# A kernel of two layers: masks added on VectorE, part of a normalisation on ScalarE

## What is computed

```python
q = _rope(qkv[:, :, :HQ], pos); k = _rope(qkv[:, :, HQ:HQ + HKV], pos); v = qkv[:, :, HQ + HKV:]
k = jnp.repeat(k, rep, axis=2); v = jnp.repeat(v, rep, axis=2)
scores = jnp.einsum('bqhd,bkhd->bhqk', q, k) * D ** (-0.5)
causal = jnp.tril(jnp.ones((s, s), dtype=bool))
scores = jnp.where(causal[None, None], scores, jnp.finfo(scores.dtype).min)
attn = jax.nn.softmax(scores, axis=-1)
out = jnp.einsum('bhqk,bkhd->bqhd', attn, v).reshape(b, s, HQ * D)
return jnp.einsum('bso,ho->bsh', out, w_o)
```

## Time and profile before

| | |
|---|---|
| median of 3 runs | 380.17 us (379.9 to 381.06) |
| profiled execution | 380.05 us, its span 378.2 us |
| granted TensorE clock | 0.999 |
| busy: TensorE, VectorE, ScalarE, GpSimd | 95%, 81%, 66%, 75% |
| chain that ended last | TensorE 80%, VectorE 11%, ScalarE 4% |

### The profile page before, as it was taken

One profiled execution on the slowest core, in us unless ns is written; L12 is line 12 of the kernel. 1 busy time (PEld: TensorE's weight loads), 2 busy tenths in 40 slices (PEclk: granted clock), 3 DMA queues, 4 the chain that ended last, 5 costly groups with the idle time before them and its releaser, 6 DMA issues.

```text
span 378.2 us, 8305 instructions
## 1 busy us (share of the span) xinstructions
PE 360.5 (95%) x2808; PEld 335.7 (89%) x2824; DVE 307.1 (81%) x684; ACT 250.7 (66%) x804; POOL 282.3 (75%) x242
## 2 busy tenths in 40 slices
PE   8999988997899999999999999999999999999995
PEld 3668878997898999999999999999999999998984
DVE  6868998866999987879878887887787878888882
ACT  1367865563987666777767586867666777767771
POOL 5537759789999999999779697777987977775000
PEclk9999999999999999999999999999999999999999
DMA  7997001523343445343345743343455433334100
GB/s 258 412 409 314 28 30 45 144 66 83 85 109 97 118 118 149 101 121 87 83 114 143 178 114 103 102 105 85 126 136 162 122 85 85 84 100 105 50 2 28
DMA packets 35371, 46.19 MB, mean 122 GB/s; under 512 B 4609, under 2 KB 27138, under 8 KB 34946
## 3 DMA queue, kind: packets, MB, share of 16 engines
q1 hardware_dynamic: 35184, 45.66, 41.8%
q10 hardware_dynamic: 146, 0.00, 0.0%
HBM read 13.14 MB, written 1.05 MB: 38 GB/s over the span
## 4 chain that ended last, share of the span: by engine, by line
PE 80%; DVE 11%; ACT 4%; DMA 2%; issue 2%; POOL 0%; SPq 0%
PE bank L1321 17%; PE bank L1033 13%; PE bank L1341 12%; PE bank L1229 12%; PE bank L1281 10%; PE bank L1188 3%; PE bank L1287 3%; PE bank L1284 2%; ACT bank L519 2%; PE bank L1164 2%; PE bank L1042 2%; DMA wq0T<-in_L_attn_w_qkv_dram 2%; PE bank L1245 2%; DVE neg_max L940 1%; PE bank L1050 1%
## 5 line engine op out<-in xcount | busy, mean ns | idle before, releaser
L519 ACT ACTIVATE bank<-bank,neg_max 128x256 f32<-128x256 f32 (+1 forms) x256 | 101.1, 396 | 10.5 <-DVE neg_max L940 10.3
L528 ACT ACTIVATE probT_hi<-bank 128x512 fp32r<-128x512 f32 x96 | 57.7, 602 | 65.0 <-PE bank L1033 64.9
L940 DVE TENSOR_REDUCE neg_max<-bank 128x2 f32<-128x512 f32 (+1 forms) x96 | 65.9, 687 | 23.6 <-PE bank L1287 13.2
L1321 PE MATMUL bank<-probT_hi,v 128*128 128x256 f32 x384 | 76.5, 295 | 0.7 <-DVE oT_lo L968 0.7
L956 DVE TENSOR_TENSOR prob<-bank,rsum 128x512 f32<-128x512 f32 x96 | 66.4, 691 | 3.3
L962 DVE TENSOR_TENSOR probT_lo<-bank,probT_hi 128x512 fp32r<-128x512 f32 x96 | 65.3, 681 | 0.5 <-ACT probT_hi L528 0.4
L681 POOL TENSOR_TENSOR rope_b<-turned,cst 128x512 f32<-128x512 f32 x36 | 46.9, 1302 | 22.1 <-DMA turned<-raw 22.1
L1281 PE MATMUL bank<-kT,qT 128*128 128x256 f32 (+1 forms) x384 | 62.6, 272 | 0.0
L1033 PE MATMUL bank<-cst,prob 128*128 128x128 f32 x384 | 57.9, 273 | 4.3 <-DVE prob L956 3.3
L1321 PEld LDWEIGHTS bank<-probT_hi,v 128*128 128x128 f32 x384 | 58.7, 189 | 3.6 <-issue 2.3
L1281 PEld LDWEIGHTS bank<-kT,qT 128*128 128x128 f32 x384 | 55.0, 191 | 0.0
(11 more groups left out here) (163 smaller groups left out, 781.7 us busy)
## 6 DMA issues: line engine op xcount, KB each, us to landing
turned<-raw SPq DMA_DIRECT2D x72, 128.0 KB, 2.0
qT<-q_hi SPq DMA_DIRECT2D x64, 128.0 KB, 2.4
qT<-split_lo SPq DMA_DIRECT2D x64, 128.0 KB, 2.4
wq0T<-in_L_attn_w_qkv_dram SPq DMA_DIRECT2D x4, 512.0 KB, 7.9
wout<-in_L_attn_w_out_dram SPq DMA_DIRECT2D x4, 512.0 KB, 12.7
nat_qkv<-in_L_attn_w_qkv_dram SPq DMA_DIRECT2D x2, 1024.0 KB, 20.4
nat_o<-in_L_attn_w_o_dram SPq DMA_DIRECT2D x1, 2048.0 KB, 21.1
kT<-split_hi SPq DMA_DIRECT2D x16, 128.0 KB, 2.4
```

The lines of the kernel that those rows point to most:

```text
L519: ins = nc.scalar.activation(own, own, ACT.Exp, bias=neg_max[it % 2][:, first + j:first + j + 1], accum_out=sums[it % 2][:, first + j:firs ...
L528: nc.scalar.activation(probT[0][:, n % 4, :], bank[2 + n % 2][:, :], ACT.Copy).then_inc(t_hi, 1)
L940: dve.tensor_reduce(neg_max[n // UNITS % 2][:, unit_columns(n % UNITS)], score_bank(n)[:, :].rearrange("p (h k) -> p h k", h=heads), AX.X, ...
L1321: ins = pe.matmul(group_bank(), v[b % 2][:, DH * z:DH * z + P], p, start=m == 0, stop=m == last)
```

## The change

The queries' rotation constants are negated, so that the scores come out negative. The maximum becomes a minimum, which needs no negation to be the exponential's bias, and the exponential takes its input with scale -1. The mask becomes +1e30. In the constants a block of zeros (C_FREE) stands ahead of the mask, so that both together are a mask of 256 columns.

For units with c = 1 TensorE's mask matmul is left out; the last scores matmul signals s_full. VectorE adds the mask itself, head by head, in place in the bank, with an instruction that also takes the minimum (`tensor_tensor_reduce`, add and min, with accumulator output). Units with c = 0 keep the mask matmul and the one reduction.

The table SHARED = (0, 4) names the units of a pass whose product with the reciprocal ScalarE does (`shares`), one instruction per head; VectorE does only the reciprocal there. `normed` is TensorE's wait for whichever engine did it.

```diff
--- before.py
+++ after.py
@@ -25,14 +25,14 @@
 EPS_LN, EPS_BIT = 1e-5, 1e-6
 EPS_RMS = float(np.finfo(np.float32).eps)
 MAGIC = 1.5 * 2.0 ** 23
-MASKED = -1e30
+MASKED = 1e30
 WQ0_PIECES = 4
 ITS = B * HKV
 UNITS = 6
 N_UNITS = ITS * UNITS
 
 
-C_ID, C_MASK, C_EVEN, C_ONE, C_QC = (P * i for i in range(5))
+C_ID, C_FREE, C_MASK, C_EVEN, C_ONE, C_QC = (P * i for i in range(6))
 C_QS, C_KC, C_KS, C_ALL = (C_QC + SEQ * i for i in range(1, 5))
 
 
@@ -49,8 +49,8 @@
     ang = np.arange(SEQ, dtype=np.float32)[None] * np.tile(np.repeat(inv, 2), P // DH)[:, None]
     sign = np.where(np.arange(P) % 2, np.float32(1), np.float32(-1))[:, None]
     cos, sin = np.cos(ang).astype(np.float32), np.sin(ang).astype(np.float32) * sign
-    c[:, C_QC:C_QC + SEQ] = cos * np.float32(DH ** -0.5)
-    c[:, C_QS:C_QS + SEQ] = sin * np.float32(DH ** -0.5)
+    c[:, C_QC:C_QC + SEQ] = cos * np.float32(-(DH ** -0.5))
+    c[:, C_QS:C_QS + SEQ] = sin * np.float32(-(DH ** -0.5))
     c[:, C_KC:C_KC + SEQ] = cos
     c[:, C_KS:C_KS + SEQ] = sin
     return c
@@ -172,6 +172,7 @@
         ld_qkv = [sem(f"ld_qkv_{i}") for i in range(3)]
         s_dve = sem("s_dve")
         yT_in, full_done, x_hi, xr_done = sem("yT_in"), sem("full_done"), sem("x_hi"), sem("xr_done")
+        s_norm_act = sem("s_norm_act")
         w_hi, w_lo = sem("w_hi"), sem("w_lo")
         root_in, root_out = sem("root_in"), sem("root_out")
         const_done = sem("const_done")
@@ -264,6 +265,16 @@
             else:
                 engine.wait_ge(raw_done, BLOCK[f] + 1)
 
+        SHARED = (0, 4)
+
+        def normed(engine, n):
+
+            upto = [m % UNITS in SHARED for m in range(n + 1)]
+            if upto[n]:
+                engine.wait_ge(s_norm_act, upto.count(True))
+            else:
+                engine.wait_ge(s_norm, upto.count(False))
+
         def unit_heads(u):
 
 
@@ -516,9 +527,22 @@
                 first = unit_columns(u).start
                 for j in range(heads):
                     own = score_bank(n)[:, wide * j:wide * j + wide]
-                    ins = nc.scalar.activation(own, own, ACT.Exp, bias=neg_max[it % 2][:, first + j:first + j + 1],
+                    ins = nc.scalar.activation(own, own, ACT.Exp, bias=neg_max[it % 2][:, first + j:first + j + 1], scale=-1.0,
                                                accum_out=sums[it % 2][:, first + j:first + j + 1])
                 ins.then_inc(s_exp, 1)
+
+            def shares(n):
+
+                act.wait_ge(rs_done, n + 1)
+                if n >= 3:
+                    act.wait_ge(t_full, n - 2)
+                _, heads, _, wide = unit_heads(n % UNITS)
+                first = unit_columns(n % UNITS).start
+                for j in range(heads):
+                    own = slice(wide * j, wide * j + wide)
+                    ins = nc.scalar.activation(prob[n % 3][:, own], score_bank(n)[:, own], ACT.Copy,
+                                               scale=rsum[n // UNITS % 2][:, first + j:first + j + 1])
+                ins.then_inc(s_norm_act, 1)
 
             def probs_T(n):
 
@@ -535,6 +559,8 @@
             def slot(n):
                 if 2 <= n < N_UNITS + 2:
                     probs_T(n - 2)
+                if 1 <= n < N_UNITS + 1 and (n - 1) % UNITS in SHARED:
+                    shares(n - 1)
                 if n < N_UNITS:
                     probs(n)
                 if group_at(n):
@@ -936,10 +962,16 @@
 
             def maxima(n):
                 dve.wait_ge(s_full, n + 1)
-                _, heads, _, _ = unit_heads(n % UNITS)
-                dve.tensor_reduce(neg_max[n // UNITS % 2][:, unit_columns(n % UNITS)],
-                                  score_bank(n)[:, :].rearrange("p (h k) -> p h k", h=heads),
-                                  AX.X, ALU.max, negate=True).then_inc(s_max, 1)
+                c, heads, _, wide = unit_heads(n % UNITS)
+                own = neg_max[n // UNITS % 2][:, unit_columns(n % UNITS)]
+                if c:
+                    for j in range(heads):
+                        part = score_bank(n)[:, wide * j:wide * j + wide]
+                        ins = dve.tensor_tensor_reduce(part, part, cst[:, C_FREE:C_FREE + SEQ], 1.0, 3e38, ALU.add, ALU.min,
+                                                       accum_out=own[:, j:j + 1])
+                else:
+                    ins = dve.tensor_reduce(own, score_bank(n)[:, :].rearrange("p (h k) -> p h k", h=heads), AX.X, ALU.min)
+                ins.then_inc(s_max, 1)
 
             def normalise(n):
 
@@ -949,6 +981,8 @@
                 par = n // UNITS % 2
                 dve.reciprocal(rsum[par][:, own], sums[par][:, own]).then_inc(rs_done, 1)
                 dve.wait_ge(rs_done, n + 1)
+                if n % UNITS in SHARED:
+                    return
                 share = rsum[par][:, own].rearrange("p (h k) -> p h k", k=1).to_broadcast([P, heads, wide])
                 if n >= 3:
                     dve.wait_ge(t_full, n - 2)
@@ -1267,7 +1301,7 @@
                 if u == 0 and g == 0:
                     has_landed(pe, BLOCK["k", b])
                 if n >= 3:
-                    pe.wait_ge(s_norm, n - 2)
+                    normed(pe, n - 3)
                 elif n == 0:
                     pe.wait_ge(f_gelu, TILES - 1)
                 elif n == 2:
@@ -1278,17 +1312,17 @@
                     pe.wait_ge(pad_zero, 2 * (b + 1))
                 for j in range(heads):
                     for s in range(c + 1):
-                        pe.matmul(ps[:, keys * j:keys * j + keys], qT[it % 2][:, h + j, P * c:P * c + P], kT[b % 2][:, g, s, 0:keys],
-                                  start=j == 0 and s == 0, stop=False, skip_group_check=True)
+                        ins = pe.matmul(ps[:, keys * j:keys * j + keys], qT[it % 2][:, h + j, P * c:P * c + P], kT[b % 2][:, g, s, 0:keys],
+                                        start=j == 0 and s == 0, stop=bool(c and s), skip_group_check=True)
                     if c == 0 and j % 2:
                         pe.matmul(ps[:, keys * (j - 1):keys * (j + 1)], q_hi[it % 2][:, (h + j) // 2, 0:P], k_pad[b % 2][:, g, :, :],
                                   start=False, stop=False, skip_group_check=True)
-                diag = ps[:, :].rearrange("p (h k) -> p h k", h=heads)[:, :, P * c:P * c + P]
-                pe.matmul(diag, ident_b[:, :], mask_b[:, 0:heads, :], start=False, stop=True,
-                          skip_group_check=True).then_inc(s_full, 1)
+                if c == 0:
+                    ins = pe.matmul(ps[:, :], ident_b[:, :], mask_b[:, 0:heads, :], start=False, stop=True, skip_group_check=True)
+                ins.then_inc(s_full, 1)
 
             def prob_T(n):
-                pe.wait_ge(s_norm, n + 1)
+                normed(pe, n)
                 if n >= 2:
                     pe.wait_ge(t_lo, n - 1)
                 elif n == 0:
```

## The result

The change is slower: 387.06 us (median of 4 runs, 386.8 to 388.13) against 380.03 us (4 runs, 379.79 to 381.06), a ratio of 1.0185, 95% interval 1.0169 to 1.0202. Predicted were 386.3 us and slower, with a range of 379.0 to 392.0. The profiled execution took 386.95 us with a span of 385.1 (before 378.2): 6.9 us to explain.

What follows compares the result with a forecast made beforehand. TensorE, busy 95% of the span, bounds the kernel, with its waits for oT_lo. Ordinary passes +1.1, k 0, v +2.6, pass 0 +1.0, pass 1 +0.6, pass 15 +0.6 and +0.4: +6.3 us, forecast 386.3, range 379.0 to 392.0.

Steps and rivals of the forecast that it cites:

- one chain in unit 5: Extreme values through shares, exponentials and oT_lo to TensorE's third head group: 3.71 us, was 2.67; growth 1.04 exceeds slack 0.73.
- k passes: Passes 5 and 9, k projection in unit 4: wait of 0.49 us against 0.48 won, net 0.
- v passes: Passes 2, 6, 10, v projection in unit 4: wait 1.33 us, net +0.85 each, +2.6 for three.
- ordinary passes: Eight passes (3, 4, 7, 8, 11 to 14): wait 0.43 us, 0.36 won, net +0.14 each, +1.1 us.
- rival 2: Chain in unit 5 shorter than worked, break-even at 3.37 us; with lower bounds -1.6 us, 378.5 us; chance 0.16.
- Extreme values: VectorE's two add-and-minimum instructions per unit: 0.37 + 0.08 us each, 0.90 for the unit, +0.31 over one reduction.
- Rival 1: VectorE's pairs of instructions don't overlap: 1.14 us instead of 0.90, +6.0 us, 392.3 us; chance 0.10.
- Shares: ScalarE's two scaled copies of 256 elements, PSUM to SBUF: 0.36 us apart, 0.72 for the pair.
- Rival 3: ScalarE's copies cost 0.45 us each: +2.9 us, 389.2 us; chance included in the forecast's 0.66.
- Passes 0 and 1: Pass 0 +1.0 us, only unit 4's mask won; pass 1 +0.6, after 0.3 off for VectorE's relief.
- shares of unit 0: ScalarE's copies in unit 1's slot, costed at nothing: done 2.3 us after the scores end, needed some 2.7 after.
- Pass 15: Last pass: wait of 0.90 us runs through to the end, +0.6 net; VectorE's lateness at unit 0's transposes +0.4.

Runs made afterwards that it cites:

- e1: The change with no shared units: VectorE does all products with the reciprocal and still adds the c = 1 masks; 379.75 us, ratio 0.998 to the kernel before.
- e4: The change with TensorE's mask matmul back in all units, units 0 and 4 still shared; 385.73 us, ratio 1.0143 to the kernel before.
- e3: The change with unit 4 alone shared on ScalarE; 385.69 us, ratio 1.0141 to the kernel before.
- e2: The change with unit 0 alone shared on ScalarE; 379.08 us, ratio 0.9976 to the kernel before.
- e8: The change with masks on VectorE only from pass 3 on and no shares on ScalarE; 377.35 us, ratio 0.9913 to the kernel before.
- e9: The full change, masks and shares, but only from pass 3 on; 381.76 us, ratio 1.0042 to the kernel before.
- e5: The change with unit 4's shares issued behind oT_hi instead of ahead of unit 5's exponentials; 383.93 us, ratio 1.009 to the kernel before.
- e6: The change with the shares of both unit 4 and unit 0 issued later in ScalarE's order; 389.94 us, ratio 1.0236 to the kernel before.

## Why the prediction came out right, and where its terms were off

**The mechanism held.** The prediction put everything on one chain in unit 5, and on the slack of 0.73 us behind it. The chain was found as written, the waits stand where they were named (unit 0 in nearly every pass, longest after a v projection), and e1, with the masks alone, has none in unit 0 of the ordinary and k passes and 0.4 us in the v passes. In ordinary passes e4, with the shares alone, has none there either: that wait takes both. Length of the chain to the start of oT_lo: before 2.10 us, predicted 3.14, measured 2.98. With oT_lo and the signal that is 3.55 us for 3.71, above the 3.37 us at which rival 2 let the change break even.

**Extreme values, 0.90 us predicted, 0.72 measured.** The term that failed is the 0.08 us for each read of the accumulator; the 0.37 for each instruction was right. In the trace a read starts together with the next instruction, and takes no time of its own: the steps are 0.34 and 0.38 us, though each instruction lasts 446 ns. Rival 1 falls with it. The Trainium skill, VectorE: DVE Perf Modes, section The DRAIN you can't avoid, has the next operation wait until the pipe is empty, and adds that one that is not held back starts earlier; here the second starts 0.08 us before the first one's end, so it is the addition that the trace agrees with. This takes some 0.2 us from each wait: 0.23 measured for 0.43 in ordinary passes, 0.31 for 0.49 in the k passes, 1.15 for 1.33 in v passes. So the ordinary passes came out at 0, not +0.14 each (0.2 us for the eight, predicted 1.1), the k passes at -0.3 for two (0), the v passes at +2.0 for three (+2.6).

**Shares, 0.72 us predicted, 0.73 measured.** Taken from the step of two exponentials' lengths, and right. The Trainium skill, ScalarE: Activation LUTs, section What ACT_TABLE_LOAD costs, gave an estimate of 0.40 us apart; the trace has 0.365, 0.73 for the pair. Rival 3, 0.45 each, falls with that.

**Passes 0 and 1, +1.6 us predicted, +3.2 measured.** The failed step is the 0.3 us "from VectorE's relief" and the silence on VectorE's own additions there. VectorE isn't relieved: its feed-forward instructions get longer, and the extreme values come late behind them. In the change, GpSimd, VectorE and ScalarE at the seam of the two passes:

```profile
109.16 1.58 DVE L1017 SCALAR_TENSOR_TENSOR x<-wcol,ffac,x 128x256 f32<-128x256 f32 x1
109.17 1.30 POOL L723 TENSOR_TENSOR split_lo<-rope_a,q_hi 128x512 fp32r<-128x512 f32 x1
...
110.67 0.42 DVE L970 CUSTOM_DVE_ANT_0 bank<-bank,cst 128x256 f32<-128x256 f32 x1
...
111.39 0.15 DVE L982 RECIPROCAL rsum<-sums 128x2 f32<-128x2 f32 x1
...
111.59 0.84 ACT L543 ACTIVATE prob<-bank,rsum 128x256 f32<-128x256 f32 x2 [1.30 <-DVE rsum L982]
```

The reciprocal of unit 0 stands behind an instruction of 1.58 us and the extreme values, and the transposes wait 1.34 us for the shares (112.48, above). That is not ScalarE's doing. In e3 VectorE makes the same product, and TensorE waits as long:

```profile
112.22 0.42 PEld L1067 LDWEIGHTS bank<-cst,prob 128*128 128x128 f32 x4 [1.33 <-DVE prob L990]
```

So the shares of unit 0, costed at nothing, cost next to nothing here too: e2 and e1 are 0.04 us apart in the two passes together, the change and e3 0.14. e1 and e2 divide the loss of 3.2 us: masks alone cost 1.85 in the two passes, with unit 0's shares it is 1.9, and unit 4's shares make up the rest.

**Pass 15, +1.0 us predicted, +0.7 measured;** the 0.4 us for unit 0's transposes didn't come.

**The last store, 0 predicted, +1.1 measured.** The prediction has no term for it.

**The total was partly luck.** Too little was forecast for passes 0 and 1 (by 1.6 us) and for the last store (1.1); too much for the ordinary passes (0.9), the v passes (0.6), the k passes (0.3) and pass 15 (0.3). That leaves 0.6 us between 6.3 and 6.9. The range, 379.0 to 392.0, would have held a kernel without any change as well; it is the terms that were tested.

## What to carry to other kernels

Before you move work to an engine that is less busy, look at what stands behind its slot in that engine's order: 0.73 us on a ScalarE that was 66% busy made TensorE wait for up to 1.3 us at a time, where 0.5 had been the longest, since it stood between a late producer and early consumers, and the fastest kernel is one with VectorE at 83%. Then ask in which stages the cover exists: the masks on VectorE won 0.27 us in an ordinary pass and lost 0.85 and 1.0 in the first two, and putting them only where they pay made 377.35 us of 380.36.

## What was not expected of the hardware

**VectorE's feed-forward instructions end with GpSimd's.** The same 256 elements from three operands in SBUF take 0.47 us at best and 1.58 at worst, and the mean of the eight moved from 829 ns (before) to 1066 (e1) with no change to them. The twelve traces hold 96 of these instructions. 85 last longer than 0.48 us, and every one of them ends 0.28 to 0.29 us after the end of a GpSimd instruction that was running when it began, or that began with it, as at the seam above: GpSimd's ends at 110.47, VectorE's at 110.75. The other 11 take 0.47 or 0.48 us, and when they began GpSimd was doing nothing or had 0.10 us or less of its instruction left. So the length says at what point of GpSimd's instruction (1.3 us and more) VectorE's happened to begin, and a change that shifts VectorE by some tenths of a us changes it. The mean is 817 to 841 ns in the four kernels with TensorE's masks in passes 0 to 2 (before, e4, e8, e9) and 1011 to 1092 in the eight others. A kernel with an idle GpSimd there was not run.

**The granted clock fell once in some executions.** In the profiles of e5 and e6 it was down for 3.4 us from about 39 us on, long before the attention passes. Windows of e5 from 35 to 45 us, then the same of e8 (window, length, then busy us (x instructions) of PE, PEld, DVE, ACT and POOL, granted clock, DMA share, GB/s):

```profile
35.00:40.00 5.00, 3.57 (x19) 2.89 (x18) 4.41 (x20) 3.88 (x8) 3.18 (x5) 0.90 0.07 30
40.00:45.00 5.00, 5.00 (x30) 4.52 (x29) 3.60 (x13) 2.69 (x6) 3.88 (x5) 0.76 0.00 0
```

```profile
35.00:40.00 5.00, 3.58 (x21) 3.03 (x20) 4.40 (x20) 3.89 (x8) 3.17 (x5) 1.00 0.08 33
40.00:45.00 5.00, 5.00 (x35) 4.46 (x35) 4.66 (x19) 4.23 (x7) 3.94 (x5) 1.00 0.07 26
```

From 35.00 us to the fall in e5, at 38.99, TensorE was busy for 2.56 us there and for 2.57 in e8, where the clock did not fall. While the clock was down, from 2.4 to 1.2 GHz, matmuls of 512 columns took 0.63 instead of 0.39 us (starts 0.43 instead of 0.23 apart), and e5 reached the start of pass 0 1.2 us later than the change (97.02 against 95.79). What sets it off stays open. The ten executions of e1 fit this: five with a mean clock of 1.000 took 378.2 to 379.3 us, five with 0.994 or 0.995 took 380.2 to 380.6. That is where e1's median, 0.4 us below that of the kernel before, parts from its profiled span, 1.2 us below.
